# Between the two layers of a graph network: rows made earlier on VectorE, Gram copies moved from ScalarE to GpSimd, and clears cut into five pieces

## What is computed

```python
h = relu(layernorm(x));  x = x + gat(h, W, att_w, src, dst)       # layer 0: attention over the edges, 8 heads of 64
h = relu(layernorm(x));  x = x + gnn(h, src, dst, ...)            # layer 1
# gnn(h):
xn   = batchnorm(h)                                  # needs sum and sum of squares of each column of h
agg  = segment_sum(xn[src], dst) / deg
conv = relu(agg @ W_conv + b_conv)
q, k, v = (h_dense @ W for W in (Wq, Wk, Wv))        # only the first 256 nodes, 8 heads of 64, random features (proj)
attn = (phi(q) @ (phi(k).T @ v)) / z @ Wo
return batchnorm(conv + attn + h)
```

## Time and profile before

| | us |
|---|---|
| median of 3 runs | 3114.46 |
| lowest, highest | 3110.58, 3115.38 |
| the profiled execution, its own time | 3113.11 |
| its span | 3111.3 |

### The profile page before, as it was taken

The page is one execution under the profiler, slowest core; times in us unless marked ns, Lnnn a source line. Parts: engine busy times, 40 slices in busy tenths (PEclk is TensorE's granted clock), DMA queues, the critical chain, the costliest instruction groups (busy, mean ns, idle before and its releaser), DMA issues. The chain is left out here.

```text
span 3111.3 us, 45478 instructions
## 1 busy us (share of the span) xinstructions
PE 2468.4 (79%) x11200; PEld 1539.0 (49%) x11201; DVE 2432.8 (78%) x4175; ACT 1040.9 (33%) x3233; POOL 1890.3 (61%) x1927
## 2 busy tenths in 40 slices
PE   1698736988989898989878899777777777779990
PEld 1355525766767676767656733333333333334440
DVE  9999998988989898988887567766666666666658
ACT  5644334555555555555546700000000000001220
POOL 0000007777777777777746467777777777775667
PEclk6799867999999999999998899999999999999995
DMA  5011027787878787877757867777777777774227
GB/s 195 32 44 44 36 72 231 235 240 234 244 235 243 229 244 236 243 235 231 243 192 257 289 184 211 210 210 210 210 210 210 210 210 210 210 211 139 64 57 283
DMA packets 227574, 601.74 MB, mean 193 GB/s; under 512 B 57441, under 2 KB 57441, under 8 KB 227481
## 3 DMA queue, kind: packets, MB, share of 16 engines
q0 software_dynamic: 136960, 456.11, 50.5%
q1 hardware_dynamic: 90520, 144.66, 13.8%
HBM read 546.53 MB, written 54.10 MB: 193 GB/s over the span
## 5 line engine op out<-in xcount | busy, mean ns | idle before, releaser
L499 POOL DMA_INDIRECT big<-feat_table,idx x880 | 840.0, 955 | 745.4 <-ACT idx L521 447.5
L1087 POOL DMA_INDIRECT big<-h_table,idx x728 | 688.5, 946 | 242.5 <-issue 211.4
L792 PE MATMUL psA<-big,onehot 128*128 128x260 f32 x1760 | 451.7, 401 | 16.0 <-DVE big L675 13.9
L792 PE MATMUL psB<-big,onehot 128*128 128x260 f32 x1760 | 434.8, 390 | 7.3
L547 ACT ACTIVATE big<-big,late_weights 128x65 f32<-128x65 f32 x1760 | 434.0, 340 | 0.0
L792 PEld LDWEIGHTS psA<-big,onehot 128*128 128x128 f32 x1760 | 325.4, 195 | 103.9 <-issue 37.0
L792 PEld LDWEIGHTS psB<-big,onehot 128*128 128x128 f32 x1760 | 318.2, 191 | 64.4 <-DVE acc L685 17.6
L521 ACT CAST idx<-minorB 128x8 int32 (+1 forms) x108 | 21.7, 203 | 910.0 <-DMA big<-h_table,idx 679.0
L1725 PE MATMUL psA<-big,onehot 128*128 128x512 f32 x488 | 241.8, 619 | 79.7 <-DMA big<-h_table,idx 50.5
L1485 DVE TENSOR_TENSOR acc<-acc,psA 128x512 f32 x278 | 190.8, 686 | 126.2 <-PE psA L1725 67.9
L1725 PE MATMUL psB<-big,onehot 128*128 128x512 f32 x488 | 236.9, 608 | 65.7 <-DMA big<-h_table,idx 44.1
(11 more groups left out here) (404 smaller groups left out, 3999.4 us busy)
## 6 DMA issues: line engine op xcount, KB each, us to landing
nodes_all<-slot_nodes SPq DMA_DIRECT2D x56, 512.0 KB, 5.7
big<-feat_table,idx POOLq DMA_INDIRECT x880, 3.8
feat_table<-big SPq DMA_DIRECT2D x49, 264.0 KB, 2.1
x_table<-acc SPq DMA_DIRECT2D x49, 256.0 KB, 4.1
big<-h_table SPq DMA_DIRECT2D x49, 256.0 KB, 2.6
big<-x_table SPq DMA_DIRECT2D x49, 256.0 KB, 4.2
acc<-in_x_dram SPq DMA_DIRECT2D x4, 3072.0 KB, 17.5
big<-in_x_dram SPq DMA_DIRECT2D x48, 256.0 KB, 4.3
```

Of the source, the lines that this page charges most:

```text
L499: g.indirect_dma_start(ring[:, b.k, q * SB + u, :], None, feat_table, bass.IndirectOffsetOnAxis(ap=idx[:, 2 * b.k + q, u:u + 1], axis=0)). ...
L792: ins = pet.matmul(psum[:, 512 * hf:512 * hf + HALF_W], onehot[:, q, u % SB, :], ring[:, b.k, u, HALF_W * hf:HALF_W * (hf + 1)], start=(u ...
L1087: g.indirect_dma_start(rows_l1[SB * r.place + b], None, h1_table, bass.IndirectOffsetOnAxis(ap=idx[:, r.place, b:b + 1], axis=0)).then_inc ...
```

## The change

1. VectorE makes more x1 slots ahead of each step of the attention: 17 slots instead of 13 before the value copies, then up to 20, 23, 24 + h//2, 28 and 29 instead of 15, 17, 18 + h//2, 22 and 23. From `x1_upto(30 + h)` on the order is as before.
2. ScalarE's roots of groups 2 and 3 move: `deviations(2)` from behind `keep_uk(1)` to between the copies of kT and projT, `deviations(3)` from behind h1(13) to behind `keep_uk(2)`, ahead of `keep_uk(3)`.
3. For tiles from 16 on (index 16, the 17th tile) ScalarE makes h1 only once, into `hout`; GpSimd copies it from there into `h1_blocks`. ScalarE waits for that copy before it reuses a `hout` buffer, SyncE before it loads `W_conv`.
4. GpSimd's two memsets are replaced. Tiles 0 to 27 are cleared in four pieces of 7 tiles (3640 columns), behind the copies of tiles 36, 38, 40 and 42. Tiles 28 to 39 (6240 columns) are cleared by ScalarE in the loop over the heads, at head 4, ahead of the copy `qfT5`.

```diff
-        BLOCKED = 3
+        BLOCKED, BLOCKED_BY_ACT = 3, 16
...
         def layer1_sync(sp):
             wait_h1_stored(sp)
+            sp.wait_ge(h1_blocked, TILES)
             sp.dma_start(Wc_s, w_by_block(W_conv)).then_inc(Wc_loaded, 16)
...
+        CLEAR_AFTER = (36, 38, 40, 42)
...
-            for n in range(2):
-                first, end = CLEARED[n:n + 2]
-                pool.wait_ge(x1_stored[n], 16 * (end - first))
-                pool.wait_ge(h1_blocked, end)
-                g.memset(acc_flat[:, first * ACC_W:end * ACC_W], 0.0).then_inc(acc_cleared, 1)
+            for t in range(BLOCKED_BY_ACT, TILES):
+                pool.wait_ge(h1_ready, t + 1)
+                pool.wait_ge(grams, t - BLOCKED + 1)
+                if t == BLOCKED_BY_ACT:
+                    pool.wait_ge(h1_blocked, t)
+                g.tensor_copy(h1_blocks[:, t % BLOCKED, :, 0:P], hout[t % KEPT].rearrange("p (k c) -> p k c", k=KD)
+                              ).then_inc(h1_blocked, 1)
+                if t in CLEAR_AFTER:
+                    n = CLEAR_AFTER.index(t)
+                    if n == 0:
+                        pool.wait_ge(x1_stored[0], 16 * CLEARED[1])
+                    first, end = (CLEARED[1] * m // len(CLEAR_AFTER) * ACC_W for m in (n, n + 1))
+                    g.memset(acc_flat[:, first:end], 0.0).then_inc(acc_cleared, 1)
...
+                if t >= BLOCKED_BY_ACT + KEPT:
+                    act.wait_ge(h1_blocked, t - KEPT + 1)
                 make_h1(hout[q], t).then_inc(h1_ready, 1)
-                if t == 0:
-                    act.wait_ge(ones_set, 1)
-                if t >= BLOCKED:
-                    act.wait_ge(grams, t - BLOCKED + 1)
-                make_h1(h1_blocks[:, t % BLOCKED, :, 0:P], t).then_inc(h1_blocked, 1)
+                if t < BLOCKED_BY_ACT:
+                    if t == 0:
+                        act.wait_ge(ones_set, 1)
+                    if t >= BLOCKED:
+                        act.wait_ge(grams, t - BLOCKED + 1)
+                    make_h1(h1_blocks[:, t % BLOCKED, :, 0:P], t).then_inc(h1_blocked, 1)
...
             done(s.mul(kT.rearrange("p k n -> p (k n)"), psC[:, :], SCALE), "kT")
+            deviations(2)
...
                 keep_uk(h)
-                if h == 1:
-                    deviations(2)
+                if h == 2:
+                    deviations(3)
             for t in range(8, 14):
                 h1_tile(t)
-            deviations(3)
...
+                if h == 4:
+                    act.wait_ge(x1_stored[1], 16 * (CLEARED[2] - CLEARED[1]))
+                    s.memzero(acc_flat[:, CLEARED[1] * ACC_W:CLEARED[2] * ACC_W]).then_inc(acc_cleared, 1)
...
-            x1_upto(13)
+            x1_upto(17)
...
-            x1_upto(15)
+            x1_upto(20)
...
-            x1_upto(17)
+            x1_upto(23)
             for h in hs:
                 max_k(h)
-                x1_upto(18 + h // 2)
-            x1_upto(22)
+                x1_upto(24 + h // 2)
+            x1_upto(28)
...
-            x1_upto(23)
+            x1_upto(29)
...
-            dve.wait_ge(acc_cleared, 2)
+            dve.wait_ge(acc_cleared, len(CLEAR_AFTER) + 1)
```

## The result

The changed kernel takes 3137.10 us (median of 4 runs, 3134.77 to 3138.17) against 3112.52 us of the kernel before in the runs beside them: a ratio of 1.0077, 95% interval 1.0060 to 1.0095. It is slower, by 24 us (19 to 30 by the interval), where no change was predicted. The profiled execution took 3137.23 us, its span is 3135.4, 24.1 more than before.

The account below looks back on a forecast made before the run. The bound was taken to be GpSimd's gather list, its 33rd gather held by the attention's chain through gram(48). Terms 0.5 + 0 + 1.8 + 0 = +2.3 us on 3114.46 gave 3116.8 us, range 3108 to 3124, "no change".

Parts of the forecast that it names:

- the frame: Between the layers: the change counts only by moving gram(48)'s end or lengthening the loop over the heads; gathers stay 1.250 us apart.
- those 46.6 us: Loop over the heads, from gram(48)'s end at 1765.02 us to TensorE's first sum; no Gram or x1 in it.
- Part (1): VectorE ahead of the value copies: four more slots, 6.1 to 9.9 us, fit into 10.48 us idle; cost 0.
- Part (2): From the lead to exp_k's table load: late root and SyncE's stop hold up slot 25; load 2.9 us late, lead gone.
- Part (3): Up to VectorE's variance of group 5: ScalarE's saved second h1 makes become idle time; 0 to 0.8 us late, 0.5 taken.
- A: Instant when VectorE's variance of group 5 ends, 1728.61 us in the kernel before; forecast 0.5 us later.
- Part (4): From the variance of group 5 to the first h1(36): same instructions and order, copy taken as 0.65 us; change 0.
- Part (5): From the first h1(36) to gram(48)'s end: GpSimd's copies and clears come first, 23.7 us instead of 21.9, +1.8.
- Part (6): Loop over the heads: ScalarE's clear of 5.3 us is covered ahead of qfT5, gathers' slack holds; 0 taken.
- R1: Rival, slower: GpSimd's copy costs like a two-input operation and bounds h1(36) to gram(48); +7.1 us, 3121.6; chance 0.10.
- R2: Rival, slower: TensorE's clock drops for the last grams after waits between clears; +5 to +9 us, say 3120.5; chance 0.18.
- R3: Rival, faster: VectorE's lead survives slot 25, variance of group 5 comes 8.6 us earlier; -6.8 us, 3107.7; chance 0.12.

Follow-up runs that it names:

- E1: Kernel before plus one GpSimd tensor_copy of a single column between the layers: 3132.96 us, ratio 1.0066.
- E2: Changed kernel with GpSimd multiplying h1 by a column of ones into the Gram blocks instead of copying: 3124.75 us, ratio 1.0043 to the kernel before.
- E9: Kernel before plus a one-column GpSimd MEMSET between the layers, repeated run: 3112.12 us, ratio 0.9997.
- E18: Kernel before with x1 slots 13 to 16 made ahead of the value copies and nothing else moved, repeated run: 3111.17 us, ratio 0.9995.
- E4: Kernel before with only the lead of x1 and the moved roots added: 3117.94 us over 10 runs, ratio 1.0019.
- E3: Changed kernel without the lead of x1 and the moved roots, GpSimd's copies and the clears kept: 3133.02 us, ratio 1.0078 to the kernel before.
- E15: Changed kernel with a GpSimd TENSOR_SCALAR (times 1.0) for the COPY: ratio 1.0098 to the kernel before, which took 3657 us in those runs.
- E11: Kernel before with the lead and moved roots, and the stores of h1(8) to h1(15) later in SyncE's list, repeated run: 3116.28 us, ratio 1.0008.
- E13: Kernel before plus a one-column GpSimd COPY behind layer 1's last gather; no usable time, the kernel before took 3657 us in those runs.

## Why the prediction was wrong

**The step that failed first is the frame**: "the change is worth what it does to the end of gram(48), plus what it adds to those 46.6 us". It took the 1.250 us between two gathers as given in both kernels, and didn't look at layer 0 at all. 16.6 of the 24.1 us lie there, 8.0 in layer 0 and 8.6 in layer 1, at 9 to 11 ns a gather in the mean. E1 gives the effect with the COPY alone, E2 takes the COPY away and the effect with it, E9 shows that it is no matter of one instruction more. Nothing in the trace of before shows this price, and no rival held it. What could have been seen is the exposure: 1,700 gathers paced by one engine, so 10 ns on each is 17 us, seven times the sum that I forecast; a new kind of instruction on that engine deserved a bound of its own on them.

**Part (1), right.** VectorE waits 3.51 us ahead of the value copies (under 4 predicted), and E18 shows the four slots at no cost.

**Part (2), right in its mechanism, mis-sized.** ScalarE's root, h1(8), SyncE's stop and VectorE's wait at slot 25 came as described, but exp_k's table load is 9.7 us late where 2.9 was the term. Less the 8.0 us of layer 0, the root is at 1684.1 (1681.9 predicted) and h1(8) at 1690.2 (1685.1). Of those 5.1 us, 2.2 are the root's and 2.9 the copies of uk: I priced them at their own duration, half of 1.07 us, and they came in rounds of 2.74 us for two, most of it TensorE's. In the kernel before such a round took 1.80 us. My own numbers could have told: uk3 at 1677.1 and h1(8) at 1681.10 are 4.0 us for the same five copies that I priced at 2.9. So 1.1 of the 2.9 us was to be seen before the run, and 1.8 came with the slower rounds. In the stretches (us, busy of the five engines with counts, granted clock, DMA share, GB/s) the reason is to be seen:

```profile
1680.00:1690.00 10.00, 8.43 (x57) 6.93 (x56) 8.79 (x13) 4.71 (x8) 10.00 (x9) 0.91 0.57 210
1690.00:1700.00 10.00, 6.73 (x20) 4.60 (x20) 3.25 (x8) 4.58 (x9) 1.73 (x2) 0.60 0.01 4
1700.00:1710.00 10.00, 5.45 (x25) 4.76 (x24) 5.81 (x12) 6.09 (x9) 0.00 (x0) 0.50 0.95 313
```

TensorE stood waiting for the copies behind the root, its granted clock fell from 0.91 to 0.60 and then 0.50, the lower of its two levels (1.2 GHz), and five feature matmuls took 2.08 us. And the DMA engines, which the lead was to fill, moved 4 GB/s for 10 us: SyncE's queue stood still from 1683.90 to 1699.08.

```profile
1683.42 0.48 SPq L474 DMA_DIRECT2D big<-in_x_dram  x1
1699.08 0.34 SPq L466 DMA_DIRECT2D h_table<-big  x1
```

**Part (3), half right.** ScalarE's saving did turn into idle time where the prediction put it (6.45 us ahead of the root of group 5 instead of 4.46). I let it absorb all but 0.5 us of the delay; it took back 3.0 of 9.7, and A is 6.7 late. The term of the sum was +0.5. How much of the 6.7 is the lead's is less sure: E4 says 3 to 9 us by itself, E3 that taking it out of the changed kernel gives nothing that the times resolve. By the ratios E1's COPY costs 20.5 us and E4's lead 5.9, together 26.4 beside the changed kernel's 24.0; the intervals allow that the two add up, and don't show it.

**Part (4), right**: A to h1(36) took 14.2 us (14.5). **Part (5), right**: the copy is 0.61 us (0.65 taken), a clear 3.13 (3.06), gram(48) ends 23.6 us behind h1(36) (23.7). (For a copy of 0.43 us the prediction gives +0.1; its terms make it +0.3.) The order of GpSimd's list is to be seen here:

```profile
1757.56 0.61 POOL L1074 COPY big<-big 128x512 f32<-128x512 f32 x1 [2.88 <-PE psB L1594]
1758.11 3.13 POOL L1081 MEMSET acc<- 128x3640 f32 x1
1761.19 1.18 POOL L1074 COPY big<-big 128x512 f32<-128x512 f32 x2
1762.32 3.13 POOL L1081 MEMSET acc<- 128x3640 f32 x1
...
1773.94 1.71 POOL L1074 COPY big<-big 128x512 f32<-128x512 f32 x3
```

The estimate from the Trainium skill ("GPSIMD Engine Reference", section 3.1) for one-input work, some 0.44 us and the dispatch, is near the COPY's 0.61 and far from the TENSOR_SCALAR's 1.49. **Part (6), right**: ScalarE's clear (5.40 us, from 1798.15) and qfT5's copy (to 1804.0) end ahead of the feature matmul that covers them (1806.4).

That the copy's 0.65 us came true is in part luck: I took it "since the copy has one input", and E15's operation has one input too and takes 1.49.

**The rivals.** R1 didn't come in the changed kernel, since the copy took 0.61 us; in E2, where it takes 1.04, it came at 7.0 us for 6.6. R2 didn't come: the last five grams took 4.52 us, as before. Its mechanism, a slower TensorE behind a wait, did strike, but between the clears, where GpSimd's list sets the pace and hides it. A gram of the chain there, at a granted clock of 0.50 (1766 to 1768.5 us):

```profile
1766.24 2.09 PE psB L1594 x8
```

It struck 60 us earlier too, in the feature matmuls, where nothing hid it. R3 fell by the argument that the prediction had against it, and in E11, where the stop for h1(8) is moved away, the lead still gains nothing that the time shows.

**What stays open** is why a COPY between the layers lengthens all gathers, those before it included, and a TENSOR_SCALAR only those behind it. The Trainium skill ("GPSIMD Engine Reference", section 2.1) describes that each instruction goes to a software dispatcher, which finds the entry for its opcode and calls it; a price that depends on the kinds of instructions would fit, but no run here shows where in a gather's 0.95 us the 7 to 14 ns lie. Also open is whether what an earlier execution leaves behind plays a part.

## What to carry to other kernels

Where one engine's list of many equal instructions sets the time, a new kind of instruction on that engine is a change to all of them: compare the mean duration and the end of the stretch that the diff doesn't touch before explaining anything behind it. A lead on one engine is worth only as much as the queue that feeds it lets through; follow every step moved (here a root) to the engine that waits behind it, and price that engine at the clock it has after a wait. And judge an edit between two paced stretches by many runs: single traces of almost the same order of work differed here by 6 us in that stretch.

## What the runs showed of the hardware

GpSimd's indirect gathers took a median of 946 ns where only MEMSETs and two-input products stood between the two layers' gathers, up to 949 in some executions; behind one TENSOR_SCALAR there they took 953 to 957; with a COPY there 953 to 960, and in layer 0, ahead of it, 953 to 957. With the COPY behind the last gather it was 946 again (949 in E13).

For 128x512 float32 GpSimd took 0.61 us for a COPY, 1.04 for a TENSOR_TENSOR with a broadcast column as its second input and 1.49 for a TENSOR_SCALAR by a constant. Of the two with a single input one is the fastest of the three and the other the slowest; I had expected them alike.
